# Expert layer by sorted lots of 128 rows for 24 of 32 token tiles, in place of all eight experts for every token

## What is computed

```python
xt = layernorm(x1)                                  # 4096 tokens of 128
scores = softmax(xt @ gate_w.T)                     # 8 experts
_, idx = top_k(scores + gate_bias, 2)
weights = take_along_axis(scores, idx, axis=1)
for e in range(8):
    gate_e = sum(where(idx == e, weights, 0.0), axis=1)
    h = silu(xt @ w1[e].T) * (xt @ w3[e].T)         # 128 -> 128
    y = y + gate_e[:, None] * (h @ w2[e].T)         # 128 -> 128
z = silu(xt @ sw1.T) * (xt @ sw3.T) @ sw2.T         # shared, 256 wide
out = x1 + y + z
```

## Time and profile before

| | |
|---|---|
| time, median of 3 runs (lowest, highest) | 773.46 us (771.48, 778.71) |
| span of the profiled execution | 770.0 us |
| PE busy, share of the span | 690.5 us, 90% |
| DVE busy | 589.2 us, 77% |
| ACT busy | 514.7 us, 67% |
| POOL busy | 255.8 us, 33% |
| first expert matmul | at 540.1 us |
| DMA moved | 138.48 MB, mean 180 GB/s |

### The profile page before, as it was taken

The page is one execution under the profiler, slowest core; times in us unless marked ns, Lnnn a source line. Parts: engine busy times, 40 slices in busy tenths (PEclk is TensorE's granted clock), DMA queues, the critical chain, the costliest instruction groups (busy, mean ns, idle before and its releaser), DMA issues. The chain is left out here.

```text
span 770.0 us, 27094 instructions
## 1 busy us (share of the span) xinstructions
PE 690.5 (90%) x10316; PEld 507.9 (66%) x10368; DVE 589.2 (77%) x2036; ACT 514.7 (67%) x1032; POOL 255.8 (33%) x253
## 2 busy tenths in 40 slices
PE   4687879899888899988999988988999999999997
PEld 3465657677666677766777766766666666666665
DVE  7965686788787788787888887977566776677676
ACT  3686967688797878888888998887335343443331
POOL 9443445334355534545543445533000000000000
PEclk9988989999999999999999999999999999999999
DMA  9899998689989778787778779841000000000000
GB/s 255 262 295 335 333 303 264 203 244 277 309 250 302 255 222 253 249 238 241 236 222 266 221 232 255 271 153 50 3 22 28 29 5 23 28 15 1 14 15 14
DMA packets 117839, 138.48 MB, mean 180 GB/s; under 512 B 8976, under 2 KB 86288, under 8 KB 117520
## 3 DMA queue, kind: packets, MB, share of 16 engines
q1 hardware_dynamic: 117712, 136.75, 58.6%
HBM read 82.26 MB, written 54.46 MB: 178 GB/s over the span
## 5 line engine op out<-in xcount | busy, mean ns | idle before, releaser
L1075 DVE CUSTOM_DVE_ANT_0 ps<-ps,near 128x128 f32<-128x128 f32 (+3 forms) x512 | 245.1, 509 | 90.5 <-PE ps L837 57.0
L998 ACT ACTIVATE work<-ps,nmin 128x128 f32<-128x128 f32 (+3 forms) x512 | 248.4, 548 | 54.2 <-DVE nmin L1075 49.4
L849 PE MATMUL ps<-ident,work 128*128 128x128 f32 x1280 | 202.6, 278 | 20.7 <-issue 11.6
L849 PEld LDWEIGHTS ps<-ident,work 128*128 128x128 f32 x1280 | 157.0, 143 | 36.5 <-issue 13.7
L795 POOL TENSOR_SCALAR_AFFINE_SELECT work<-work 128x512 f32<-128x512 f32 x96 | 61.5, 641 | 237.8 <-ACT work L987 203.6
L1392 ACT ACTIVATE near<-ps 128x512 f32<-128x512 f32 x80 | 47.5, 595 | 133.3 <-PE ps L1357 133.2
L799 POOL TENSOR_TENSOR work<-work 128x512 f32<-128x512 f32 x96 | 124.2, 1294 | 8.0
L1060 DVE COPY work<-ps 128x512 f32<-128x512 f32 (+1 forms) x192 | 123.2, 642 | 2.5 <-issue 1.6
L837 PE MATMUL ps<-kb,qb 128*128 128x384 bf16 (+3 forms) x460 | 110.6, 298 | 12.3 <-ACT work L998 9.4
L1367 PEld LDWEIGHTS ps<-work,near 128*128 128x128 f32 x640 | 82.6, 192 | 34.2 <-issue 31.6
L987 ACT ACTIVATE work<-ps 128x512 f32<-128x512 f32 (+1 forms) x160 | 90.2, 564 | 18.7 <-PE ps L849 18.1
(11 more groups left out here) (111 smaller groups left out, 627.3 us busy)
## 6 DMA issues: line engine op xcount, KB each, us to landing
near<-w_slots SPq DMA_DIRECT2D x96, 512.0 KB, 5.4
w_slots<-relS SPq DMA_DIRECT2D x128, 256.0 KB, 4.5
qk_rows<-work SPq DMA_DIRECT2D x36, 256.0 KB, 4.7
near<-w_slots SPq DMA_DIRECT2D x32, 256.0 KB, 4.6
qk_rows<-y SPq DMA_DIRECT2D x9, 256.0 KB, 6.8
qb<-qk_rows SPq DMA_DIRECT2D x24, 96.0 KB
kb<-qk_rows SPq DMA_DIRECT2D x24, 96.0 KB
qb<-qk_rows SPq DMA_DIRECT2D x48, 48.0 KB
```

Source lines behind the costliest of these rows:

```text
L849: ins = nc.tensor.transpose(tp_ps[:, m % 2, n * P:(n + 1) * P], prob[:, m % PROBS, n * P:(n + 1) * P], ident[:, :])
L998: ins = nc.scalar.activation(prob[:, m % PROBS, h * wide:(h + 1) * wide], qk_ps[:, m % 3, h * wide:(h + 1) * wide], ACT.Exp, bias=nmin[:, ...
L1075: nc.vector.tensor_tensor_reduce(out=scores, in0=scores, in1=near[:, q % NEAR, a, 4 * P - wide:4 * P, r], scale=1.0, scalar=3e38, op0=ALU. ...
```

## The change

The first three groups (24 tiles, 3072 tokens) are no longer given to all experts. Their rows are normalised by POOL, their gates are made by DVE during slots 310 to 325 (48 operations, most of them on 128x192 or wider), and places in a list sorted by expert are counted (`place`). POOL then scatters each row twice into the DRAM tensor `sent`: 48 indirect DMAs of 128 rows, three behind each of the quads 120 to 126 and 27 behind the last. Each expert's part of the list is rounded up to lots of 128 rows. 56 lots in 14 groups of four are loaded again by SP, transposed, multiplied by the weights of their lot's expert (the offset is read into a register of PE from a table), transposed, multiplied by w2, and stored to `made`. 48 indirect DMAs fetch the results back, and DVE adds them with their weights (`mix`). `sent` is cleared before by 14 DMAs of 256 KB in slots 188 to 227. The last eight tiles are computed by all experts as before, in two chunks. The order at the end is: six chunks with the shared halves alone (`last_row` within them), 14 groups of sorted lots, two chunks with all experts.

```diff
+CT = CH // P                # 4
+RT = TILES - GB * NI        # 24
+RCH = RT // CT              # 6
+LOTS = (TOPK * RT * P + E * (P - 1)) // P
+GROUPS = (LOTS + CT - 1) // CT      # 14
+ROW0 = [FIRST[QUADS * (GI - NI + k)] for k in range(NI)]     # 264, 296, 304, 320
+TURN_SLOT = [ROW0[0] + 7 + 3 * j for j in range(RCH - 2)] + [ROW0[1] + 6, ROW0[1] + 9]
+COUNT_SLOT = ROW0[1] + 25
+ROOTS_AT = [ROW0[0] - 24, SLOT_OF["pj", GI - NI - 1] + 2]     # 240, 295
+CLEAR_AT = [ROW0[0] - 76 + 3 * k for k in range(GROUPS)]
+GATES_AT = SLOT_OF["lg", RCH - 1] + 1                          # 310
+PLACE_AT = SLOT_OF["px", 0] + 1                                # 323
@@ gpsimd, behind near_probs(q)
+                    for k in range(TOPK * RT):
+                        if q == SENT_BEHIND[k]:
+                            route["send"](pool, k)
+                experts["pool"](pool)
@@ scalar
-                    if m == FIRST[NQ - QUADS] + 8:
-                        experts["roots"](act, 0)
-                    if m == NU:
-                        experts["normalise"](act, 0)
+                    for k in range(2):
+                        if m == ROOTS_AT[k]:
+                            route["roots"](act, k)
@@ expert_part
+    def send(pool, k):
+        nc.gpsimd.indirect_dma_start(out=sent[:, :], out_offset=bass.IndirectOffsetOnAxis(ap=index[:, k:k + 1], axis=0),
+                                     in_=xnr[:, k % RT, :], in_offset=None).then_inc(sent_out, 16)
+    def pool_program(pool):
+        for n in range(2):
+            pool.wait_ge(ys_out[n], 16 * GROUPS // 2)
+        for j in range(RCH):
+            for n in range(CT * j, CT * (j + 1)):
+                for r in range(TOPK):
+                    nc.gpsimd.indirect_dma_start(out=back[:, r, n, :], ..., in_=made[:, :], ...).then_inc(back_in[j // 2], 16)
+        def lots(k):
+            return [pe.value_load(lot_at[0:1, CT * k + n:CT * k + n + 1], min_val=0, max_val=(E - 1) * WE) for n in range(CT)]
+        def hidden_sent(k, at):
+            pe.wait_ge(xsT_done, k + 1)
+            wait(pe, s_done, 2 * (k - 1))
+            for n in range(CT):
+                ins = nc.tensor.matmul(hs_ps[k % 2][:, n // 2, (n % 2) * 2 * P:(n % 2 + 1) * 2 * P],
+                                       xsT[:, k % 2, n * P:(n + 1) * P], we_flat[:, bass.ds(at[n], 2 * P)], start=True, stop=True)
+        for k in range(GROUPS + 2):
+            if k < GROUPS:
+                hidden_sent(k, at[k])
+            if k + 1 < GROUPS:
+                at[k + 1] = lots(k + 1)
...
+            if 1 <= k <= GROUPS:
+                turn_hidden(k - 1)
+            if k >= 2:
+                product_sent(k - 2, at[k - 2])
+            if k + 1 < GROUPS:
+                turn_sent(k + 1)
@@ DVE, sorted lots: products of k (two halves), then
+            if k >= 2:
+                dve.wait_ge(ys_ready, k - 1)
+                nc.vector.tensor_copy(ys[:, k % 2, :], ys_ps).then_inc(ys_done, 1)
+            if k + 1 < GROUPS:
+                copy_sent(k + 1)                                # xT_ps -> xsT
@@ DVE, last two chunks (k - S counts the 20 steps)
+        def mix(j):
+            dve.wait_ge(back_in[j // 2], 16 * 2 * TOPK * CT)
+            ...                                                # 8 scalar_tensor_tensor of 128x128
+            if (k - S) % 3 == 2 and k - S >= 5:
+                mix((k - S) // 3 - 1)
+        for j in range((DCH * NM) // 3 - 1, RCH):
+            mix(j)
```

More of the change, by code:

```diff
@@ L1207, in prepared_at @@
-    def prepared_at(j):
-        late = LATE if j == 1 else 0
-        base = NM * (j - 1) + late
-        return {"normalise": base - late + 1, "turn": base + 2, "copy": base + 3, "scores": base + 4, "shift": base + 5,
-                "exp": base + 6, "softmax": base + 7, "pick0": base + (8 if j > 1 else 7),
-                "pick1": base + (9 if j > 1 else 8)}
-    def due(step, what):
-        return [j for j in range(1, CHUNKS) if prepared_at(j)[what] == step]
+    sent_tiles = sent.rearrange("(n p) c -> p n c", p=P)
@@ new lines, in additions, with tensor_program, hidden, product @@
+    def additions(k):
+        return AC * (k // NY) + 1 + CT * (k % NY) if k >= 0 else 0
+    def tensor_program(pe, last_row, last_row_read):
+        def hidden(k, first, third, rhs):
+            wait(pe, silu_done, k - 1)
+            wait(pe, hT_done, k - 1)
+            nc.tensor.matmul(h1_ps[k % 2], first, rhs, start=True, stop=True).then_inc(h1_ready, 1)
+            nc.tensor.matmul(h3_ps[k % 2], third, rhs, start=True, stop=True).then_inc(h3_ready, 1)
+        def product(bank, ks, weights):
+            pe.wait_ge(hT_done, ks[-1] + 1)
+            for n in range(CT):
+                for k, w in zip(ks, weights):
+                    ins = nc.tensor.matmul(bank[:, n * P:(n + 1) * P], hT[:, k % 4, n * P:(n + 1) * P], w,
+                                           start=(k == ks[0]), stop=(k == ks[-1]))
+            ins.then_inc(y_ready, 1)
+        shared = [ws[:, m, 2 * P:WE] for m in range(NSH)]
+        def shared_product(c):
+            wait(pe, add_done, c)
+            product(y_ps[0], [NSH * c, NSH * c + 1], shared)
+        for k in range(S):
+            c, m = divmod(k, NSH)
@@ L1353, in hidden @@
             if m == 0:
                 pe.wait_ge(xnT_done, c + 1)
-            wait(pe, silu_done, k - 1)
-            wait(pe, hT_done, k - 1)
-            nc.tensor.matmul(h1_ps[k % 2], w1_sb[:, m, :], rhs, start=True, stop=True).then_inc(h1_ready, 1)
-            nc.tensor.matmul(h3_ps[k % 2], w3_sb[:, m, :], rhs, start=True, stop=True).then_inc(h3_ready, 1)
-        def product(c, u):
+            hidden(k, ws[:, m, 0:P], ws[:, m, P:2 * P], xnT[:, c % 2, :])
+            if m == 0 and c:
+                shared_product(c - 1)
@@ new lines, in tensor_program, with turn_sent @@
+            last_row(k)
+            if m == 0 and c + 1 < RCH:
+                turn_tiles(pe, c + 1)
+        shared_product(RCH - 1)
+        last_row_read(pe)
+        def turn_sent(k):
+            pe.wait_ge(xs_in[k % 3], 16 * (k // 3 + 1))
+            if k == 0:
+                pe.wait_ge(xnT_done, RCH)
+            wait(pe, xsT_done, k)
+            for n in range(CT):
+                ins = nc.tensor.transpose(xT_ps[:, n * P:(n + 1) * P], xs[:, k % 3, n, :], t["ident"][:, :])
+            ins.then_inc(xsT_ready, 1)
@@ L1370, in product @@
-            ins.then_inc(y_ready, 1)
-        for c in range(CHUNKS):
+            base = S + NM * c
+            if u == 0:
+                product(y_ps[k % 2], [base, base + 1], shared)
+            else:
+                product(y_ps[k % 2], [base + u + 1], [we[:, u - 1, 2 * P:WE]])
+        for c in range(DCH):
             for m in range(NM):
-                step = NM * c + m
-                hidden(c, m)
+                w = ws[:, m, :] if m < NSH else we[:, m - NSH, :]
+                if m == 0 and c == 0:
+                    pe.wait_ge(s_done, 2 * GROUPS)
+                hidden(S + NM * c + m, w[:, 0:P], w[:, P:2 * P], xnTd[:, c, :])
@@ L1376, in tensor_program @@
                 if m == 0 and c:
[L1377 removed]
+                    dense_product(c - 1, NY - 1)
                 if m >= 2:
[L1379 to L1385 removed]
+                    dense_product(c, m - 2)
+        dense_product(DCH - 1, NY - 1)
@@ L1403, in vector_program, with hidden @@
+        for k in range(S, S + DCH * NM):
+            silu_of(k)
     def vector_program(dve, last_row):
-        def hidden(c, m):
-            k = NM * c + m
+        def hidden(k):
             dve.wait_ge(silu_done, k + 1)
@@ L1508, in twice, with beside @@
         return placed
-    hidden = lambda shared, experts: np.concatenate([shared.reshape(NSH, P, C), experts]).transpose(2, 0, 1)
+    def beside(first, third, second):
+        return np.concatenate([first.transpose(2, 0, 1), third.transpose(2, 0, 1), second.transpose(2, 0, 1)], axis=2)
+    halves = lambda w: w.reshape(NSH, P, C)
     arrays = {
```

758 lines of the change are left out of this document (525 added, 233 removed).

## The result

| | before | after |
|---|---|---|
| time, median of 4 runs each (lowest, highest) | 772.84 us (771.48, 778.71) | 878.17 us (872.86, 883.95) |
| ratio, 95% interval | | 1.132, 1.1225 to 1.1423 |
| span of the profiled execution | 770.0 us | 871.1 us |
| PE busy | 690.5 us, 90% | 655.1 us, 75% |

A forecast was written before the change was run, and what follows sets the result against it. It took the expert part as bound by PE's columns and the attention by engines waiting for each other. Experts 39 + 80 + 70 = 189 against 229.9 (-41), attention +27, so -14: 760 us, range 730 to 806.

The forecast's parts named there:

- POOL's 27 remaining scatters lie beside it: Shared chunks: POOL's scatters left after the last quad run alongside the predicted 39 us, adding nothing.
- 48 X: Last two chunks: the 48 gathers gate the steps and take 48 us, plus 21.7 for the rest, 70 in all.
- X: POOL's time for one indirect DMA of 128 rows, in no profile row, taken as 1.0 us between 0.37 and 1.29.
- The rival of dear transfers: Indirect DMAs cost POOL more: gain gone from 1.2 us each, total 781 at 1.29, about 802 at 1.5; chance 0.22.
- the last step's 5: Shared chunks: 5 us for the attention's last step, counted within the predicted 39.
- The turn: Sorted groups: time from one group to the next, 5.2 us, 14 of them making 73 of the stage's 80.
- the wait for DVE's copies: Sorted groups: PE idles 1.05 us per group while DVE makes two PSUM copies, giving 4.6 us before register loads.
- the register load: Sorted groups: four loads into PE registers at 0.58 us each, mostly under queued matmuls, 0.6 us a group uncovered.
- The gates: Attention, slots 310 to 325: 48 DVE operations of 16.5 us, some 3 in idle time: +13.5, and +3.5 beside POOL.
- the lock: Attention: 27 gate operations of DVE meet POOL on SBUF, +3.5 us; 10.6 by the skill's rule; rival of worst blocking 0.05.
- roots 3: Attention: one root on ACT goes and two come, in slots 240 and 295, about 2.9 us each: +3.
- that rival: Sorted groups: PE's clock falls in half the groups, +25 us, total 785; chance 0.13 shared with wholly unhidden register loads.

The follow-up runs named there:

- e1: Changed kernel with its 48 scattering indirect DMAs replaced by plain DMAs of the same size issued by SP: 829.08 us.
- e8: Kernel before plus 48 back-to-back indirect DMAs on POOL in the expert stage that nobody waits for: 820.57 us against 778.39.
- e3: Changed kernel with all 96 indirect DMAs replaced by plain DMAs of the same size, still issued by POOL: 770.33 us.
- e4: Changed kernel with each lot's expert a constant instead of a number loaded into a PE register: 856.81 us.
- e15: Kernel before plus 48 indirect DMAs nobody waits for, one small memset behind each (pitch 1.42 us): 809.54 us against 771.54.
- e10: Changed kernel with one small memset on POOL behind each of the last 27 scatters and the 48 gathers: 823.89 us.
- e13: Changed kernel with one memset behind each late scatter and gather, and two of four register loads per group moved behind the next transposes: 827.96 us, ratio 1.071.
- e6: Changed kernel with five small memsets on POOL behind each of the last 27 scatters and the 48 gathers: 915.31 us.

## Why the prediction was wrong, point by point

**The step that failed** is "POOL's 27 remaining scatters lie beside it", and with it the term 48 X of the last chunks: the sum counted an indirect DMA as POOL's time alone. Its price for POOL was nearly right: X was taken as 1.0, POOL is busy 0.95 and the pitch is 1.26. What no term and no rival had is that, back to back, they stop PE, ACT and DVE. That is 35 us of the shared chunks (81.6 against 46.6 in e1), and in the last chunks 112.7 against some 79 that by estimate a pitch of 1.25 gives without a hold-up (48 x 1.25 + 19), so about 34. In the kernel before, the same 48 DMAs cost 52.6 us (e8). The rival of dear transfers ran by arithmetic on X (781 at 1.29) and would have come out near 777; it missed the mechanism, and with it some 100 us.

**X as a pitch.** I sized POOL's work and left out the 0.30 us between two DMAs. For the last chunks alone this is 12 us (48 x 0.25); the rest of the term, 21.7, measured 19.

**The shared chunks without the hold-up** took 46.6, not 39: a chunk took 5.7, as predicted, but the first three steps, where `last_row` hangs on POOL's last quads, took 17.7 (569.2 to 586.9 in e3), where 1.5 chunks and the last step's 5, in all 13.5, were counted; the wait for the first lots is another 3.

**The turn** of 5.2 was 6.41. PE's own 3.5 (3.8 in e4's turn) and the wait for DVE's copies (1.05 predicted, 1.08 measured) were nearly right. The term that failed is the register load: I took 0.58 each from three times the smallest DVE operation, and 0.6 in all uncovered; the four take 2.9 us (0.95 and three of 0.63 to 0.67), and 1.4 to 1.7 stay uncovered (e4). The cover, 1.72 us of queued matmuls in the sum, was about right: the first load began at 732.14, and the matmuls lasted until 733.76, 1.62 us. 14 x 1.2 is 17; 7 came back, since the first two turns were shorter (4.6 and 5.7) and filling and draining overlapped with the neighbours.

**The attention**: 46 instead of 27. The gates were right in size (15 against 17 with the lock, 12.5 shown by leaving them out), and so was reading as a small price for DVE beside POOL. The rest up to slot 310 was predicted at 11 (roots 3, transposes and scores 5, DMA and SP's wait 3) and is 20.6; of the surplus 6.5 goes with POOL's normalisation, which the sum had at nothing because POOL is idle two thirds of the time. It is idle, but its own copies queue behind a block of 6.2 us, and DVE waits for them. The scatters cost 11.6 instead of 1: the pitch of 1.26 is above the 1.04 up to which they were to be hidden, and part is probably the hold-up. The sum also had the clock at nothing here. In the kernel before, PE's clock was at 1.00 through slots 264 to 351; in the changed kernel it was at 1.2 GHz for 37.5 of their 161 us, behind stretches in which PE worked 4.49 of 6.9 us (459.0 to 465.9) and 3.06 of 6.8 (503.5 to 510.3). What this cost by itself no run shows.

**PE's clock** was at 1.00 through the sorted groups, so that rival was wrong there. It fell to 0.50 (1.2 GHz) where the hold-up left PE idle, from 592 to 628 us, as a consequence and not a cause: in e8 PE stood still from 594.3 on and the clock fell at 599.1. The whole shared stage of e3 had 0.93. The sum missed the clock in the attention, as above.

**The sign.** Without indirection and register loads the change gives 770 to 752, 18 us, where the sum said 14 with both. The saving in PE's columns was real, and POOL's instruction gave it back several times over.

**The 2.0 us of the Trainium skill.** They stood beside the sum as a time of 850 if each of POOL's DMAs held POOL so long (the Trainium skill, DMA: Bandwidth & Descriptors, "Anatomy of one DMA"). The traces bear out the reading as latency: POOL itself is busy 0.95 us with an indirect and 0.545 with a plain one, and a plain one of 64 KB lands 2.3 us after its issue (e3). That the total, 878, came out nearer to 850 than to 760 has another cause.

## What to carry to other kernels

Indirect DMAs in a row had a price for the whole core here, not for POOL alone: count them (not their rows), keep them 1.8 us or more apart, and fill the gap with other POOL work. Before costing a transfer as hidden, ask what the engines share besides data: a queue whose price is known in time on its own engine can still stop the others. A load into a register of the engine that does the matmuls cost about 0.65 us of its queue; put it where that engine waits anyway. And an idle engine is not free cover if a block of work on it delays its next short answer. Compare stages, not single totals, where an untouched stage varies by more than the effect.

## What the runs showed of the hardware that I had not expected

- Of indirect DMAs at a pitch of 1.25 us the first ten or eleven do no harm (e8, and the fetches of the changed kernel); then PE, ACT and DVE are held almost entirely (13.27 us of PE in 53), until 5 to 11 us after the last began; at 1.42 PE is held about half of the time; at 1.83 the shared steps lose 1.5 us, and at 1.89 PE loses nothing. Plain DMAs of POOL at 0.53 us do no such thing, nor do SP's. The number of rows (32 or 128) changes neither the price by more than 10% nor the effect.
- The DMA engines are not full: they were 15% busy in the standstill (the last of the stage rows above), and the scatters' own packets kept moving. Whether SP's DMAs are held too is not shown; of its loads only 0.05 MB were left by 592.5. Even matmuls without a wait come a few at a time, about 0.7 us or a multiple of it apart. The trace of the changed kernel has no transfer of instructions (queues q8 and q14) between 592.6 and 629.1 us, but in e15's slow stretch such transfers do run (606.4, 614.7 and 625.3). Whether instructions, signals or something beneath both run short, and which of these is only a consequence, stays open: no run here tells them apart.
- For the scatters the threshold lies between 1.51 and 1.83 us, and near it the loss varies: 13 us over the shared steps in e10 at 1.51, 22 in e13 at the same pitch (against the 41.7 of e6). For fetches it lies lower or is not the same thing: at 1.42 they cost 36.5 us beside a PE that was never idle (e15), at 1.49 nothing beside one that waited for them (e10). Whether the pitch or the other engines' load makes this difference was not tested.
